# Addresses modulo 256 bytes for the operands of TensorE in a two-layer graph kernel

## The reference

```python
def layer0(x, adj):                       # graph attention twice, then a feed-forward net
    h = gat(gat(x, W1, a1), W2, a2)       # softmax of masked leaky_relu scores, times h @ W
    h = layernorm(x + h)
    return layernorm(h + relu(h @ w_ff1 + b_ff1) @ w_ff2 + b_ff2)

def layer1(src, adj):                     # 8 heads, 4 edge kinds, each kind with its own Wv
    q, k = src @ Wq + bq, src @ Wk + bk
    attn = softmax(q k^T / sqrt(32))
    out = sum((attn * (adj == r)) @ (src @ Wv[r] + bv[r]) for r in range(4))
    x = layernorm(src + out @ Wo + bo)
    return layernorm(x + gelu(x @ W1 + b1) @ W2 + b2)
```

## The kernel before

| product | stationary | streaming | columns | matmuls in a loop step |
|---|---|---|---|---|
| `pe_down` l=0 and 1 | hid | down_w0, down_w1 | 256 | 96 |
| `pe_up` l=0 | up_w0 | hT0 | 256 | 48 |
| `pe_up` l=1 | up_w1 | hT2 | 256 | 48 |
| `pe_qk` | q_w, k_w | hT1 | 256 | 24 |
| `pe_gat_mix`, second attention | att_s | wh | 256 | 12 |
| `pe_gat_mix`, first attention | att_s | wh | 258 | 12 |
| `pe_gat_rows`, `pe_gat_cols` | gT | gat_w | 260 | 12 |
| `pe_v` | hT1 | v_w | 512 | 12 |

## Time and profile before

### The profile page before, as it was taken

The page is one execution under the profiler, slowest core; times in us unless marked ns, Lnnn a source line. Parts: engine busy times, 40 slices in busy tenths (PEclk is TensorE's granted clock), DMA queues, the critical chain, the costliest instruction groups (busy, mean ns, idle before and its releaser), DMA issues.

```text
span 3145.6 us, 78504 instructions
## 1 busy us (share of the span) xinstructions
PE 3038.5 (97%) x26980; PEld 2743.2 (87%) x26980; DVE 2225.3 (71%) x4975; ACT 2431.9 (77%) x6218; POOL 1880.5 (60%) x1747
## 2 busy tenths in 40 slices
PE   5799999999999999999999999999999999999997
PEld 5788888888888888889889889889889889889885
DVE  4567677777777777777777777777777777777763
ACT  3578878878878778778778787787787787787774
POOL 3365665665665665665665665666666666666664
PEclk8999999999999999999999999999999999999998
DMA  4000100100100100100100100100100100100100
GB/s 143 25 22 24 33 27 23 33 27 23 33 27 23 33 27 23 33 27 23 33 27 23 33 27 23 33 27 23 33 27 23 33 27 23 33 26 24 33 12 14
DMA packets 101943, 93.54 MB, mean 30 GB/s; under 512 B 14736, under 2 KB 101008, under 8 KB 101776
## 3 DMA queue, kind: packets, MB, share of 16 engines
q1 hardware_dynamic: 101904, 93.00, 9.8%
HBM read 76.17 MB, written 16.78 MB: 30 GB/s over the span
## 4 chain that ended last, share of the span: by engine, by line
PE 91%; DVE 7%; issue 1%; ACT 1%; POOL 0%; DVEq 0%; DMA 0%; POOLq 0%; SPq 0%; ACTq 0%
PE ps_f L288 11%; PE ps_f L289 10%; PE ps_f L290 10%; PE ps_ao L485 7%; PE ps L475 6%; PE ps L288 5%; PE ps L289 5%; PE ps L290 5%; PE ps L465 4%; PE ps_ao L288 4%; PE ps_ao L530 4%; PE ps_g L288 3%; PE ps_g L289 3%; PE ps_g L290 3%; PE ps_ao L289 3%; PE ps_ao L290 3%
## 5 line engine op out<-in xcount | busy, mean ns | idle before, releaser
L1024 POOL TENSOR_TENSOR hid_lo<-hid_full,hid_hi 128x512 fp32r<-128x512 f32 x512 | 674.0, 1317 | 406.7 <-ACT hid_hi L646 387.5
L288 PE MATMUL ps_f<-down_w_hi,hid_hi 128*128 128x256 f32 x2048 | 590.4, 288 | 1.2 <-POOL hid_lo L1024 0.9
L1001 POOL TENSOR_TENSOR rstd<-vareps,neg_half 128x2 f32<-128x2 f32 x256 | 218.1, 852 | 611.9 <-DVE vareps L819 611.9
L289 PE MATMUL ps_f<-down_w_lo,hid_hi 128*128 128x256 f32 x2048 | 572.8, 280 | 0.0
L290 PE MATMUL ps_f<-down_w_hi,hid_lo 128*128 128x256 f32 x2048 | 572.6, 280 | 0.0
L663 ACT ACTIVATE prob<-ps,s_least 128x256 f32<-128x256 f32 x1024 | 468.6, 488 | 6.1 <-DVE s_least L867 5.2
L867 DVE TENSOR_REDUCE s_least<-ps 128x4 f32<-128x1024 f32 x256 | 309.4, 1209 | 141.1 <-PE ps L465 141.1
L288 PEld LDWEIGHTS ps_f<-down_w_hi,hid_hi 128*128 128x128 f32 x2048 | 385.1, 188 | 23.2 <-issue 19.9
L289 PEld LDWEIGHTS ps_f<-down_w_lo,hid_hi 128*128 128x128 f32 x2048 | 386.0, 188 | 0.0
L290 PEld LDWEIGHTS ps_f<-down_w_hi,hid_lo 128*128 128x128 f32 x2048 | 384.7, 188 | 0.0
L646 ACT ACTIVATE hid_hi<-hid_full 128x512 fp32r<-128x512 f32 x512 | 323.4, 632 | 16.7
(11 more groups left out here) (158 smaller groups left out, 9436.3 us busy)
## 6 DMA issues: line engine op xcount, KB each, us to landing
adj_in<-adj_keys SPq DMA_DIRECT2D x128, 256.0 KB, 2.8
xT_in<-x_features SPq DMA_DIRECT2D x64, 256.0 KB, 2.8
norm<-x_nodes SPq DMA_DIRECT2D x64, 256.0 KB, 2.7
out_nodes<-norm SPq DMA_DIRECT2D x64, 256.0 KB, 2.2
row_vectors<-all_row_vectors SPq DMA_DIRECT2D x1, 1536.0 KB, 11.7
raw_up<-L_w_ff SPq DMA_DIRECT2D x1, 1024.0 KB, 8.2
raw_down<-L_w_ff SPq DMA_DIRECT2D x1, 1024.0 KB, 10.7
raw_v<-L_Wv SPq DMA_DIRECT2D x4, 256.0 KB, 10.6
```

The costliest lines, as they stand in the source:

```text
L288: nc.tensor.matmul(ps_out, left[0], right[0], start=first, stop=False)
L289: nc.tensor.matmul(ps_out, left[0], right[1], start=False, stop=False)
L1024: pool.tensor_tensor(hid[1][:, 2 * m:2 * m + 2, :], hid_full[:, 2 * m:2 * m + 2, :], value(hid[0][:, 2 * m:2 * m + 2, :]), ALU.subtract).t ...
```

## The change

The tiles are declared in another order and with other fillers; no instruction, operand, wait or order is touched on any engine. `ROW` is now 64 columns, 256 bytes. `half_row` becomes `rest_of_row(n, quarters)`, a filler of 64 bytes times `quarters`. `WIDE` becomes 320 columns (1280 bytes, five times 256), so that k=0 and k=1 of gat_w and wh stand at the same place modulo 256. v_w is declared first, and the stationary weights up_w, q_w and k_w move behind the streaming ones gat_w, down_w and o_w.

```diff
-        ROW, HALF = 32, 16
+        ROW = 64
         WIDE = -(-WX // ROW) * ROW
 
-        def half_row(n):
-            return sb(f"half_row{n}", [P, HALF])
-
-        up_w = [pair(f"up_w{l}", [P, C, U]) for l in range(2)]
-        q_w, k_w = pair("q_w", [P, C, D]), pair("k_w", [P, C, D])
+        def rest_of_row(n, quarters):
+            return sb(f"rest_of_row{n}", [P, quarters * ROW // 4])
+
         v_w = pair("v_w", [P, C, R * D])
-        half_row(0)
+        rest_of_row(0, 1)
         gat_w = tuple(t[:, :, 0:WX] for t in pair("gat_w", [P, C, WIDE]))
         down_w = [pair(f"down_w{l}", [P, UC, D]) for l in range(2)]
         o_w = sb("o_w", [P, C, D])
+        rest_of_row(1, 1)
+        up_w = [pair(f"up_w{l}", [P, C, U]) for l in range(2)]
+        q_w, k_w = pair("q_w", [P, C, D]), pair("k_w", [P, C, D])
...
         ident = sb("ident", [P, P])
-        half_row(1)
+        rest_of_row(2, 2)
...
         att_s, score = staged_pair("att_s", "score", [P, C, N])
-        half_row(2)
+        rest_of_row(3, 3)
         wh = tuple(t[:, :, 0:WE] for t in pair("wh", [P, C, WIDE]))
```

## The result

The kernel after the change takes 3144.81 us (median of 16 runs, 3138.11 to 3146.49), the kernel before beside it 3151.2 us (16 runs, 3147.68 to 3153.43). The ratio is 0.9976, with a 95% interval of 0.9968 to 0.9983: faster by 5 to 10 us, at the edge of what can be told from no change. The forecast was 3134, so 17 us were expected and some 7 came. The time lies inside the range of 3098 to 3166.

A forecast was written before the change was run, and what follows sets the result against it. TensorE, busy 97%, was taken as the bound, through its matmul step. Per loop step 0.36 + 0.01 - 0.10 = 0.27 us gained, times 62 makes 17 us: 3134 us against 3150.95, range 3098 to 3166.

The forecast's parts named there:

- What bounds the kernel: TensorE is busy 97% of the span; the change can act only through the matmul step, start to start.
- Two cadences, of which one holds until something breaks it: Float32r matmuls of 256 columns step at 117.8 or 113.3 ns, until a wait or another kind of work.
- A chain of k=1 alone could thus go on at 115.6: In wh, k=1 at distance 192 averaged 115.6 ns against 117.8; 163 matmuls per loop step would gain 0.36 us.
- the second rival: Nothing changes: the steady cadence at distance 192 is near 117 ns, gains and losses cancel, 3151 us; chance 0.20.
- The loss in up l=0: 44 matmuls per loop step at 113.3 ns would come to 115.6, losing 0.10 us.
- Gains of the wide products: 12 matmuls of k=0 with 258 and 260 columns gain at most 0.03 us per loop step, taken as 0.01.
- Plain float32 at no cost: Transposes and plain float32 products stay at 109 and 215 ns; 0.4 us, 24 us in all, if wrong.
- The setup: First 100 us, clock 0.86, half at the lower clock where the array sets the steps: no gain counted there.
- The slower rival, loss per load: Each stationary load loses 17.5 ns, so 256-column chains step at 126.7 ns: 3278 us; slower 0.22, strong form 0.10.
- the 3191 of its half: Half the loss per load: steps of 120 ns, 0.65 us more per loop step, 3191 us.
- The quick cadence everywhere: 163 matmuls per loop step fall to 113.3 ns; with the wide ones 0.80 us, 50 us in all, 3101; chance 0.20.
- The rule of two read ports: Loading weights takes no read bandwidth from the running matmul; by it no layout matters and time stays at 3151.

The follow-up runs named there:

- the lone chains: Changed kernel plus chains of 13 float32r matmuls on TensorE after the last store: 1.61 us per chain at distance 64, 1.58 to 1.62 at 192, 1.64 at 0.
- the distances exchanged: Changed kernel with rows of 288 columns again for wh and gat_w, so k=1 stands at distance 64 and k=0 at 192: 3137.45 us, ratio 0.9961.

## Why the prediction was off

- **What bounds the kernel.** Right. TensorE had 97% before and after, and the one wait in the loop stayed at 0.6 us. The step start to start is all that the change could move.
- **Two cadences, of which one holds until something breaks it.** Right, and it is the heart of the case; the lone chains show both with nothing else running. That they come from the load of the next matmul meeting the streaming read of this one is an explanation that no run isolates; the runs show only that the addresses of both operands count.
- **"A chain of k=1 alone could thus go on at 115.6."** This step failed, and the sum hung on it. 163 x 2.2 = 0.36 us per loop step were expected, and the products that hold these matmuls gave 0.07: two groups of 12 went to 113.3 (0.087 us), the others stayed at 117.8, and the second attention lost 0.013. The means 116.7, 115.8, 114.2 of k=1 were three values of a passage (no steady chain of full loads at 192 shows 115.6, and with the distances exchanged the attention took 1.417 us): the chain came from distance 64 and went back to it, and the pattern repeated because the disturbance did. With one distance throughout there is no passage, and the attention went from 1400 to 1413 ns. I had written that the fall within the triple could go further; that it might not be a state at all stood under the second rival, "the saving of k=1 would be one of a transition". For the long chain this rival was right, with its 1.41 us, though by another argument than the values (117 ns). That the time still fell, as forecast, was luck: it came from two groups in the quick cadence, which the forecast did not count on.
- **The loss in up l=0.** 44 x 2.3 = 0.10 us was charged for coming to 115.6. The products stayed at 113.3; the loss was 0.02. In sum, 0.27 us per loop step were forecast and 0.033 measured in the profiled executions, 2.5 us over the loop instead of 16.
- **Gains of the wide products.** +0.01 forecast; first attention and gat_w lost 20 ns together.
- **Plain float32 at no cost, also at distance 128.** Right: eight transposes of prob 873 ns, eight of o_w 1725 ns in after, as in the earlier trace rows.
- **The setup.** Right that steps there did not change while the clock was low: eleven steps of the first wh chain take 2.50 us before and after, ten of them 215 ns each. But the 0.86 that I read the earlier trace rows is too high: the trace of before gives the clock as 1.00 there (34 to 37 us), that of after as 0.50 for the same steps. I also left out the draining, where the clock moved the time by more than a us (above).
- **The slower rival, loss per load.** Wrong: a load of 32 columns at distance 192 has the same 113.3 ns as a full one, and with full loads no steady step there is above 117.8. A kernel near the 3191 of its half does exist, 3186 at distance 0, with the 120.0 ns named there.
- **The quick cadence everywhere.** Wrong of the change, but reachable: with one transpose the long chain runs at 1.36 us as it said. What lacks to its 3101 are the products that then fall into 117.8.
- **The rule of two read ports.** The Trainium skill, TensorE: Matmul & The Clock Gate, "Step-by-step: what each phase is for", says that loading the next weights takes no read bandwidth from the running matmul. What I drew from it, that no layout would matter, does not hold for float32r: 113.3, 117.8 or 120.0 ns for the same work, by nothing but addresses and entries. Whether it is read bandwidth that the two share is not shown.

What stays open. The profiled executions differ by 1.4 us, the medians by 6.4. The runs of after spread over 8.4 us, those of before over 5.8, and the median of before was 3152.49, 3150.77 and 3155.67 us beside the three sets of experiments; for this reason each kernel is given by its ratio to the runs of before beside it. One group of 12 in the other cadence is 12 x 4.4 ns x 60 = 3.2 us, so the spread is that of two or three groups, and the kernel with the transpose shows such alternation inside one execution: its 36 steps of down l=0 at 113.3 in some loop steps and 117.8 in others. That the missing 5 us come from such groups is likely but was not traced. Nor is it known what makes two cadences, or what in an entry chooses between them.

## What to carry to other kernels

Before building on an average step of a few matmuls, ask whether it is a state or a passage: only a long chain with the same addresses throughout shows a steady step, and even that may have two. Where TensorE is the bound with float32r, measure a few distances between stationary and streaming tiles (of the four tried in the kernel 0 was the worst and 192 the best) and, as a second knob, one useless instruction ahead of the longest chain. In the new layout one transpose was worth 0.8%, and the layout alone 0.2%; the same transpose in the old layout, and 16 columns in the new one, made the kernel slower, so each has to be tried. And with such a bistable stream, a difference of 0.2% between two kernels says where chains landed, so compare steps, chain by chain.

## What the runs showed of the hardware

- A float32r matmul of 256 columns, in an unbroken row with full loads, has two steady steps, 113.3 and 117.8 ns, with the same operands and addresses; what comes ahead of the chain decides which, mostly within five steps, and it was held for 96 matmuls. A stretch of another width or distance inside a chain can change it (down l=1, 117.8 ahead of gat_w and 113.4 behind it in the kernel with rows of 288 columns).
- The steady step depends on the address of the streaming operand beyond the stationary one modulo 256 bytes: with full loads 0 gives 120.0 ns, 64 and 192 the two above, 128 an uneven 118.6; 16 and 112 came to 113.3 or 113.4 in one of four chains each. With the streaming operand fixed and the stationary one moved, six matmuls of 512 columns took 1.461 to 1.487 us. Plain float32 stays at 109 ns per transpose and 216 per pass of 256 columns at every distance seen.
- One transpose that nobody reads made the kernel 0.8% faster than the change alone (3119.74 against 3144.81 us).
- A plain float32 matmul of 16 columns between attention and product took 0.244 us from its start to the next one's, more than the 0.084 of a full transpose at the same place.
